# The first feature table written by GpSimd in blocks of 128 rows instead of by SyncE

## The reference, cut to what matters

```python
h = jnp.maximum(_layernorm(x, axis=-1), 0.0)
x = x + _L0_gnn_ref(h, edge_index, edge_attr3_1x20, edge_weight1, ...)
# in _L0_gnn_ref:
h = x @ W_in
Wij = ssp(f_ij[:, 0, :] @ W_f1 + b_f1) @ W_f2 + b_f2
x_ij = h[idx_j] * Wij * f_ij_cutoff
agg = jax.ops.segment_sum(x_ij, idx_i, num_segments=n_atoms)
out = ssp(agg @ W_o1 + b_o1) @ W_o2 + b_o2
```

## Time and profile before

| | us |
|---|---|
| median of 2 runs (5152.11 and 5152.26) | 5152.18 |
| the profiled execution | 5143.11 |
| its span, first to last instruction | 5141.0 |
| GpSimd busy | 3665.2 (71%) |
| TensorE busy, weight loads busy | 3958.1 (77%), 3536.6 (69%) |
| VectorE busy | 3037.7 (59%) |
| ScalarE busy | 1656.6 (32%) |
| mean granted TensorE clock | 0.848 |

### The profile page before, as it was taken

One profiled execution on the slowest core, in us unless ns is written; L12 is line 12 of the kernel. 1 busy time (PEld: TensorE's weight loads), 2 busy tenths in 40 slices (PEclk: granted clock), 3 DMA queues, 4 the chain that ended last, 5 costly groups with the idle time before them and its releaser, 6 DMA issues.

```text
span 5141.0 us, 88720 instructions
## 1 busy us (share of the span) xinstructions
PE 3958.1 (77%) x26176; PEld 3536.6 (69%) x26176; DVE 3037.7 (59%) x11144; ACT 1656.6 (32%) x3637; POOL 3665.2 (71%) x3340
## 2 busy tenths in 40 slices
PE   2767677676766538888888788887888998698897
PEld 2656566565555537777777687777777887588886
DVE  3655555555554267777777766666555555355554
ACT  3444444444443234444444433332211111011110
POOL 0788888888888147777777467777577777577776
PEclk9877777777777868888888799999899999799998
DMA  6666666666665522222222222222444444444443
GB/s 215 136 113 117 114 117 120 111 120 114 116 112 71 113 60 56 60 60 57 57 57 57 50 69 60 59 59 59 143 138 134 134 136 151 145 153 154 156 160 104
DMA packets 412954, 541.52 MB, mean 105 GB/s; under 512 B 139471, under 2 KB 324408, under 8 KB 405944
## 3 DMA queue, kind: packets, MB, share of 16 engines
q0 software_dynamic: 199680, 221.72, 23.7%
q1 hardware_dynamic: 178524, 289.13, 17.8%
q10 hardware_dynamic: 34396, 26.36, 1.7%
HBM read 383.80 MB, written 153.13 MB: 104 GB/s over the span
## 4 chain that ended last, share of the span: by engine, by line
PE 47%; DMA 17%; issue 16%; POOL 10%; DVE 6%; ACT 2%; DVEq 1%; SPq 1%; POOLq 0%; ACTq 0%
DMA sums<-G,idx 15%; POOL sums L870 10%; PE psC L1410 9%; PE psF L1410 9%; PE psA L1331 5%; PE psD L1392 4%; PE psE L1392 4%; PE psA L1378 4%; PE psB L1378 4%; PE psC L1341 4%; DVE mc_mx L1821 1%; ACT arena L1081 1%; PE psE L1353 1%; PE psD L1346 1%; DMA stage<-table 1%
## 5 line engine op out<-in xcount | busy, mean ns | idle before, releaser
L846 POOL DMA_INDIRECT G<-table,idx x1664 | 1592.7, 957 | 626.4 <-issue 585.3
L870 POOL DMA_INDIRECT sums<-G,idx x832 | 1283.7, 1543 | 327.1 <-issue 203.2
L827 POOL DMA_INDIRECT G<-table,idx x832 | 785.7, 944 | 291.5 <-issue 269.7
L1113 ACT COPY arena<-psA 128x600 f32<-128x600 f32 x312 | 205.9, 660 | 1136.4 <-PE psA L1378 1127.0
L2229 DVE TENSOR_SCALAR S<-iota,dloc,ew 128x128 f32<-128x128 f32 x1144 | 318.0, 363 | 406.1 <-PE psE L1392 222.4
L1281 PE MATMUL psE<-arena,stage 128*128 128x128 f32 x832 | 210.8, 433 | 435.3 <-ACT G L1030 435.1
L1281 PEld LDWEIGHTS psE<-arena,stage 128*128 128x128 f32 x832 | 180.6, 320 | 519.9 <-ACT G L1030 519.9
L1410 PEld LDWEIGHTS psC<-arena,stage 128*128 128x128 f32 x3822 | 483.9, 193 | 45.0 <-issue 29.4
L1410 PE MATMUL psC<-arena,stage 128*128 128x144 f32 (+1 forms) x3822 | 493.1, 284 | 26.5 <-DMA arena<-adjacency 15.2
L1738 DVE TENSOR_TENSOR arena<-psB,G 128x1024 f32<-128x1024 f32 x104 | 127.4, 1225 | 641.8 <-PE psB L1262 641.8
L1410 PEld LDWEIGHTS psF<-arena,stage 128*128 128x128 f32 x3822 | 478.1, 191 | 15.0 <-issue 0.2
(11 more groups left out here) (293 smaller groups left out, 8105.9 us busy)
## 6 DMA issues: line engine op xcount, KB each, us to landing
adjacency<-arena SPq DMA_DIRECT2D x26, 2400.0 KB
arena<-adjacency SPq DMA_DIRECT2D x26, 2400.0 KB
acc<-in_src_row SPq DMA_DIRECT2D x104, 512.0 KB
arena<-in_dst_row SPq DMA_DIRECT2D x104, 512.0 KB
G<-table,idx POOLq DMA_INDIRECT x2496
sums<-G,idx POOLq DMA_INDIRECT x832
sums<-arena ACTq DMA_DIRECT2D x4, 3300.0 KB, 36.2
table<-cut ACTq DMA_DIRECT2D x147, 64.0 KB
```

Source lines behind the costliest of these rows:

```text
L827: pool.indirect_dma_start(G[st.r][:, t * width:(t + 1) * width], None, tables[n], bass.IndirectOffsetOnAxis(ap=idx[st.r][:, t:t + 1], axis ...
L846: pool.indirect_dma_start(G[at.r][:, t * D:(t + 1) * D], None, tables[n], bass.IndirectOffsetOnAxis(ap=idx[at.r][:, t:t + 1], axis=0)).the ...
L870: pool.indirect_dma_start(sums_dram[t % SUMS], bass.IndirectOffsetOnAxis(ap=idx[st.r][:, t:t + 1], axis=0), G[st.r][:, t * TW:(t + 1) * TW ...
L1113: A.copy(dense_at(at.g, m.loaded + j, at.place), counts_in((c * m.built + j) % 2)).then_inc(mixed["kept"], 1)
```

## The change

GpSimd writes blocks 0 to 47 of the first table, one indirect DMA for each block of 128 rows; the row numbers (`node_rows`, block number x 128 + partition) are made by one iota in the memory of `positive`, a tile that is used much later. GpSimd waits for each batch of `stage` as SyncE did. SyncE writes only block 48 and the padding rows, both after the last batch. The completions of the 48 writes are counted on the four `mrows` semaphores, 12 writes each; the later users of these count from 12 on. SyncE's first window load and GpSimd's first scatter wait for them too.

```diff
-        self.rows0 = before.rows0 + before.thin * (chunks // ROWS) if before else 0
+        self.rows0 = before.rows0 + before.thin * (chunks // ROWS) if before else chunks_before
...
+        node_rows = positive[:, :].bitcast(I32)
...
-        TABLE_DMAS = [NJ + 1, NJ + 3, 2 * NJ + 3, 3 * NJ + 3, 4 * NJ + 3]
+        TABLE_DMAS = [2] + [4 + q * NJ for q in range(4)]
+        SCATTERED = BLOCKS // ROWS
...
-            write_table(0)
+            reached(sp, nd[0]["rows"], NJ)
+            sp.dma_start(tables[0][(BLOCKS - 1) * P:NPAD, :], stage[:, (BLOCKS - 1) * D:BLOCKS * D]).then_inc(table_out, 16)
 
             sp.dma_start(tables[0][NPAD:ACC, :], stage[:, 0:D]).then_inc(table_out, 16)
             sp.wait_ge(pro["flag"], 1)
...
                 if not st.general and isinstance(st.c, int) and st.c == 0:
                     sp.wait_ge(table_out, 16 * TABLE_DMAS[0])
+                    for q in range(ROWS):
+                        sp.wait_ge(mrows[q], 16 * SCATTERED)
...
-            pool.wait_ge(pool_consts, 5)
+            pool.iota(node_rows, pattern=[[P, BLOCKS]], base=0, channel_multiplier=1).then_inc(pool_consts, 1)
+            pool.wait_ge(pool_consts, 6)
             pool.affine_select(out=ident[:, :], in_=ident[:, :], compare_op=ALU.not_equal, fill=1.0, base=0,
                                pattern=[[-1, P]], channel_multiplier=1).then_inc(pool_consts, 1)
+            for b in range(SCATTERED * ROWS):
+                if b % BJ == 0:
+                    reached(pool, nd[0]["rows"], b // BJ + 1)
+                    pool.sem_inc(turns, 1)
+                pool.indirect_dma_start(
+                    tables[0], bass.IndirectOffsetOnAxis(ap=node_rows[:, b:b + 1], axis=0),
+                    stage[:, b * D:(b + 1) * D], None).then_inc(mrows[b % ROWS], 16)
             pool.wait_ge(pro["to_reduce"], 1)
             pool.partition_all_reduce(viol[:, 1:2], viol[:, 0:1], P,
                                       bass.bass_isa.ReduceOp.max).then_inc(pro["reduced"], 1)
...
             pool.wait_ge(table_out, 16 * TABLE_DMAS[0])
+            for q in range(ROWS):
+                pool.wait_ge(mrows[q], 16 * SCATTERED)
+                pool.sem_inc(turns, 1)
```

More of the change, by code:

```diff
@@ L80, with __init__ @@
 class Mix:
-    def __init__(self, n, dense, loaded, stored, counts, chunks, before):
+    def __init__(self, n, dense, loaded, stored, counts, chunks, before, chunks_before):
         self.n, self.dense, self.loaded, self.stored, self.counts = n, dense, loaded, stored, counts
@@ L140, in build_program @@
     for n, what in ((2, (3, 0, False, True)), (3, (2, 0, True, False)), (4, (3, STORED, False, False))):
-        mixes[n] = Mix(n, *what, CHUNKS, mixes.get(n - 1))
+        mixes[n] = Mix(n, *what, CHUNKS, mixes.get(n - 1), BLOCKS // ROWS)
     assert BLOCKS % BJ == 0 and CHUNKS % ROWS == 0 and CHUNKS % GROUP == 0
@@ L1217, in batch_products @@
                 ins.then_inc(s["prod"].sem, 1)
-            pe.wait_ge(pool_consts, 6)
+            pe.wait_ge(pool_consts, 7)
             pe.wait_ge(pro["columns"], 1)
@@ L1520, in _ @@
             dve.wait_ge(loaded, 16 * (len(LOADS) + 1 + (REST > 0)))
-            dve.wait_ge(pool_consts, 6)
+            dve.wait_ge(pool_consts, 7)
             link(V.tensor_copy(dst[:, :], dst_i[:, :]))
```

## The result

| | before | after |
|---|---|---|
| median of 2 runs, us | 5152.18 | 5196.43 (5194.14 to 5198.73) |
| the profiled execution | 5143.11 | 5198.73 |
| its span | 5141.0 | 5196.7 |
| first scatter of the first layer | 137.93 | 179.37 |

The ratio is 1.0084, with a 95% interval of 1.0064 to 1.0104: 44.3 us slower, less than 2% and clear of no change. A second measurement gave 1.0090 (1.0073 to 1.0107), 5199.59 against 5154.88 us.

The account below looks back on a forecast made before the run. No engine bounds the whole program; it is a row of stages. Last write at 138.9, code load, all-reduce and flag put the first edge load at 150.9 instead of 107.34: 5152.2 + 43.5 = 5195.7 us, range 5180 to 5226.

Parts of the forecast that it names:

- The path: Opening to first layer: 48 GpSimd writes delay the all-reduce, flag and SyncE's edge loads, shifting everything behind by 43.5 us.
- code load and gap: GpSimd, between last write and all-reduce: configuration change loses its cover, 8.4 us idle, plus 0.3 us queue gap.
- its end to first edge load: Behind the all-reduce: flag cast and semaphore 0.2 us, then SyncE's flag load to first edge load 1.97 us.
- nearest to the gather: GpSimd's table writes: each priced like an indirect gather of 128 rows, 0.94 us, 1.25 us from start to start.
- the rival in which VectorE holds GpSimd up: Opening, 79 to 107 us: GpSimd stands still while VectorE is busy, +11 us on the sum, 5207 us; 3%.
- The rival without a code load on the path: Ahead of the all-reduce: the sum less 8.4 us, +35 us, 5187 us; 15%.
- Each later stage as long as before: From the first scatter on: no later stage changes its length, so nothing takes back or adds to the 43.5 us.
- the layer's length: First layer: a change in its own length was named as a sign that the forecast is wrong.
- All hidden: GpSimd's idle time before the first scatter: it hides the writes, cost 1 us, 5153 us; 4%.
- A write at a scatter's price: GpSimd's table writes: 1.85 us each, last ending at 167.7, +72 us, 5224 us; 20%.
- A write that waits for the one before: GpSimd's table writes: each waits for the previous landing, 3.6 us each, +156 us, 5309 us; 2%.
- TensorE's clock: Ahead of the first layer: TensorE idles longer but starts at a low clock already; cost 0, at most 3 us.

Follow-up runs that it names:

- half dose: Changed kernel with GpSimd writing 24 blocks and SyncE 25 in four DMAs: 5170.61 against 5154.88 us for the kernel before, ratio 1.0035.
- reload: Changed kernel with an unread all-reduce at about 10 us and a one-column iota between writes and viol's all-reduce: 5215.84 against 5162.67 us for the kernel before.
- early all-reduce: Changed kernel plus one all-reduce of a constant column behind affine_select, at about 10 us, result unread: 5219.84 us, 20 above the changed kernel.
- SyncE's order changed: Kernel before with edge loads ahead of SyncE's last table writes: four chunks' edges 5160.04 against 5161.38 us, two chunks' 5155.58 against 5162.75.

## Why the prediction was right, point by point

*The path.* It came out as written: 48 writes, then the all-reduce, then the flag, then SyncE's edge loads. The opening's last part moved as a block, and no other engine filled the gap. The half dose shows that it is the number of writes that sets it.

*The terms.* Against 41.4 us for the start I had 43.5; the second profiles put the measured shift anywhere from 38.8 to 42.2. The terms differ by more than the sum and partly cancel: the last write ended 1.7 us later than expected, and what stands behind it took 4.2 us less.

| | expected | measured |
|---|---|---|
| first write starts | 79.2 | 78.66 |
| last write ends | 138.9 | 140.63 |
| code load and gap | 8.7 | 6.08 |
| all-reduce | 1.03 | 0.38 |
| its end to first edge load | 2.3 | 148.40 - 147.09 = 1.3 |

The write at 958 ns was nearest to the gather, as chosen, 1.26 from start to start. The first seven took 89.17 - 78.66 = 10.5 us instead of 8.8. In the kernel with the all-reduce first, where the writes begin at 90.09, only the first is long (1.31 us) and all others are 0.95 or 0.96; so there may be a little of the rival in which VectorE holds GpSimd up, or of first calls, 1.7 us in all. Which of the two was not tried.

*The code load.* The step was right and its size too large, 8.4 for 5.8 to 6.1. I took it from the load ahead of the first iota, which is of another code (7.80 us in the profile after, 7.48 when it was loaded again in the middle of the program), so it was the wrong row to take. The Trainium skill (GPSIMD Engine Reference, Instruction dispatch) gives 5.95 us for such a load, and the trace agrees: 6.08, 5.95 and 5.89 us ahead of the all-reduce in the changed kernel, the half and the reload. The rival without a code load on the path is refuted by those rows and by the early all-reduce, which took 4.8 us off the start.

*"Each later stage as long as before"* was the one step that failed. The scatter's median went from 1542 to 1547 ns, at most 832 x 5 ns = 4 us. With it 41.4 + 4 = 45 us stand against 44.3 and 44.7 measured. No run resolves these 4 us: the interval of the first result alone reaches from 33 to 54 us, and the unchanged kernel's first layer took 1560.8 us in one profile and 1567.6 in the other. For the same reason the layer's length, which I had named as a sign of being wrong, was no usable sign. So the path and the writes were right by reasoning, and that 43.5 fell within 1 us of the medians owes something to luck: the start was put 2.1 us too high, and this small cost later on was left out.

*The rivals.* All hidden: the start was at 179, not 138. A write at a scatter's price: 958 ns, not 1542. A write that waits for the one before: no such wait in the 48 rows. Had the change been made with the all-reduce first, as the order argument seems to ask, it would have been dearer and not cheaper: SyncE's queue alone kept the start at 175, and some 20 us lie behind the start.

*The chances.* The cases within two per cent add up to 98, not 97, so that with the 1% for faster all of them come to 101. Nor are two per cent what a measurement can tell from no change: 0.8% was clear.

*TensorE's clock.* It was granted 0.50, the 1.2 GHz level, from 107 to 151 us, all of which TensorE was idle. From the landed edges to the first scatter it was 179.37 - 155.63 = 23.7 us both then and before (137.93 - 114.18 = 23.8), so the longer idle time cost nothing that these rows show.

## What to carry to other kernels

Look at what stands behind a moved piece of work in program order, on its own engine and on the queue of whoever waits for it: an idle engine is free only up to the next instruction that somebody needs. A transfer queue that waits for one thing holds back all that needs nothing; put loads without a condition ahead of the one that waits, but no more of them than the queue drains before the next urgent transfer. And after a change on GpSimd compare the medians of its unchanged instructions before explaining anything else.

## What the hardware showed that I had not expected

The time that GpSimd needs for an indirect DMA depends on which DMA comes first after the last change of its configuration. Medians in ns, in all profiles of the kind:

| first DMA after the last code load | scatter | gather | last passes, first to last gather, us |
|---|---|---|---|
| scatter, none before the load (before, twice) | 1542 | 944 | 2173.9, 2175.2 |
| scatter, writes before the load (after twice, half) | 1547 | 944 | 2172.2, 2172.7, 2170.2 |
| scatter, writes before a second load (reload) | 1547 | 944 | 2177.8 |
| scatter, SyncE's order changed (two kernels) | 1542 | 944 | 2172.9, 2174.3 |
| indirect write (48, 36 or 4 of them) | 1552 to 1554 | 952 | 2182.7 to 2188.2 |
| indirect gather (4) | 1553 | 952 | 2185.9 |
| plain write (4) | 1543 | 955 | 2188.8 |

The change in level is small for one DMA, but the program has some 3300 of them: four extra DMAs ahead of them cost 21.2 and 17.8 us, not far from half of what the whole change cost. Only in the last passes do the levels stand apart in every profile, 2170.2 to 2177.8 us against 2182.7 to 2188.8. In the first layer (1560.8 to 1574.1 against 1569.3 to 1583.0) and in layer two (1056.5 to 1068.4 against 1062.0 to 1075.6) they overlap. Where the code comes to lie in GpSimd's memory might explain it, but nothing here shows that; what is shown is that four DMAs off everybody's path bring the dear level, and that in the kernel with 48 writes a new code load behind them takes it away.
